# Four one-row products on four column tiles instead of one, and their copy in four pieces

## What is computed

```python
def _L1_attn_ref(x, Wq, bq, Wk, bk, Wv, bv):
    q = jnp.einsum('bsd,de->bse', x, Wq) + bq
    k = jnp.einsum('bsd,de->bse', x, Wk) + bk
    v = jnp.einsum('bsd,de->bse', x, Wv) + bv
    scores = jnp.einsum('bqd,bkd->bqk', q, k) / jnp.sqrt(jnp.asarray(d, x.dtype))
    attn = jax.nn.softmax(scores, axis=-1)
    return jnp.einsum('bqk,bkd->bqd', attn, v) + x
```

## Time and profile before

| | us |
|---|---|
| median of three runs | 3160.8 |
| lowest and highest | 3159.92, 3165.76 |
| the profiled execution, whole | 3153.07 |
| its span in the trace | 3151.5 |

### The profile page before, as it was taken

How to read it: one execution, slowest core, us unless ns; L and a number is a source line. 1 busy time by engine, 2 the same in 40 slices (tenths; PEclk the granted TensorE clock), 3 DMA queues, 4 the chain that set the end, 5 groups by cost and what they waited for, 6 DMA issues and landing times.

```text
span 3151.5 us, 69490 instructions
## 1 busy us (share of the span) xinstructions
PE 2865.8 (91%) x25025; PEld 1321.0 (42%) x25025; DVE 2418.2 (77%) x3155; ACT 2122.8 (67%) x3837; POOL 614.6 (20%) x493
## 2 busy tenths in 40 slices
PE   3788888888886899999999999999999999999997
PEld 3344444444443434343344344343343443443446
DVE  6788888888883887787787887877877877877844
ACT  2477767767764567776777777777777777777762
POOL 0344444444442010110110110100100101101100
PEclk6799999999998899999999999999999999999997
DMA  3000000000002901011011010010110110110003
GB/s 89 1 16 15 15 15 15 10 15 15 15 16 98 293 1 22 1 22 23 1 22 23 1 22 19 5 22 3 21 22 2 22 22 1 23 22 1 1 1 83
DMA packets 93922, 81.85 MB, mean 26 GB/s; under 512 B 62452, under 2 KB 83541, under 8 KB 92629
## 3 DMA queue, kind: packets, MB, share of 16 engines
q1 hardware_dynamic: 92085, 78.26, 9.5%
q10 hardware_dynamic: 1568, 0.04, 0.0%
HBM read 39.57 MB, written 32.11 MB: 23 GB/s over the span
## 4 chain that ended last, share of the span: by engine, by line
PE 67%; issue 11%; ACT 7%; POOL 6%; DVE 5%; DMA 2%; ACTq 1%; POOLq 0%; SPq 0%; DVEq 0%
PE ps L1635 19%; PE ps L1607 18%; PE ps L1659 17%; POOL arena L544 4%; PE ps L1669 3%; PE ps L1619 2%; POOL arena L550 2%; ACT arena L699 1%; PE ps L1487 1%; ACT L725 1%; ACT arena L817 1%; PE ps L1714 1%; DMA arena<-in_x 1%; POOL arena L560 1%; DVE arena L1052 1%
## 5 line engine op out<-in xcount | busy, mean ns | idle before, releaser
L1211 DVE TENSOR_REDUCE arena<-ps 128x2 f32<-128x896 f32 (+1 forms) x1408 | 1456.9, 1079 | 383.4 <-PE ps L1607 383.1
L837 ACT ACTIVATE arena<-ps 128x512 f32<-128x512 f32 (+1 forms) x2464 | 1281.3, 603 | 357.8 <-PE ps L1635 348.7
L1635 PE MATMUL ps<-arena 97*128 97x512 f16 (+1 forms) x2800 | 813.8, 357 | 13.5 <-ACT arena L817 10.6
L1607 PE MATMUL ps<-arena 96*128 96x448 f16 x2800 | 774.8, 359 | 21.5 <-issue 10.8
L1659 PE MATMUL ps<-arena 128*32 128x512 f32 (+2 forms) x7328 | 667.7, 457 | 0.7 <-DVE arena L1233 0.7
L1635 PEld LDWEIGHTS ps<-arena 97*128 97x128 f16 (+1 forms) x2800 | 252.2, 99 | 436.5 <-ACT arena L837 158.1
L1659 PEld LDWEIGHTS ps<-arena 128*32 128x32 f32 x7328 | 234.7, 109 | 411.3 <-ACT arena L837 195.6
L1607 PEld LDWEIGHTS ps<-arena 96*128 96x128 f16 x2800 | 224.1, 99 | 313.3 <-DVE arena L1211 130.9
L609 POOL TENSOR_TENSOR tok<-arena,tok 128x128 f32 (+3 forms) x112 | 47.4, 423 | 1574.6 <-DVE arena L1233 1574.6
L550 POOL TENSOR_TENSOR arena<-arena 113x784 f32<-113x784 f32 x128 | 192.4, 1503 | 429.5 <-DVE arena L1061 429.5
L544 POOL TENSOR_TENSOR arena<-arena 113x784 f32<-113x784 f32 x128 | 192.3, 1502 | 129.1 <-DVE arena L1052 129.1
(11 more groups left out here) (181 smaller groups left out, 2783.1 us busy)
## 6 DMA issues: line engine op xcount, KB each, us to landing
arena<-qk_scratch SPq DMA_DIRECT2D x96, 196.0 KB, 3.8
qk_scratch<-arena SPq DMA_DIRECT2D x16, 448.0 KB, 5.0
arena<-ximg SPq DMA_DIRECT2D x16, 400.0 KB, 6.7
arena<-in_x SPq DMA_DIRECT2D x4, 1568.0 KB, 8.3
xa_scratch<-arena SPq DMA_DIRECT2D x32, 196.0 KB, 1.9
res_scratch<-arena SPq DMA_DIRECT2D x32, 196.0 KB, 2.1
arena<-xa_scratch SPq DMA_DIRECT2D x4, 1568.0 KB, 8.0
arena<-res_scratch SPq DMA_DIRECT2D x4, 1568.0 KB, 11.7
```

What stands on the lines that cost most here:

```text
L837: act.activation(pk[0:rows, x % DEPTH, QC * m:QC * m + n], ps[0:rows, w % SB, 0:n], ACT.Exp, scale=float(C) ** -0.5).then_inc(att["exp"], 1)
L1211: dve.tensor_reduce(mxp[0:rows, p, 2 * u:2 * u + k], ps[0:rows, at_:at_ + k, 0:KN], AX_X, ALU.max)\
L1607: last = pe.matmul(ps[0:rows, MB + 2 * (j % 2) + n % 2, 0:KN], q2[p][0:96, T * t:T * t + rows], k2[p][0:96, KN * m:KN * m + KN], start=Tru ...
L1635: last = pe.matmul(ps[0:rows, bank, at_ % QC:at_ % QC + chunk_cols(c)], k2[p][0:97, T * t:T * t + rows], q2[p][0:97, QC * c:QC * c + chunk ...
```

## The change

The four products of a chunk no longer start at partition 96 all. Product i of four goes to partition 32 i, that is, to column tile i, in the same bank and the same columns as before. The row of maxima is then spread over four partitions, 0, 32, 64 and 96, with 128 columns in each, and ScalarE copies it in four instructions of 128 columns, each from its partition to partition 96 of `q2`. ScalarE waits once, ahead of the first, for the same signal `mrow` as before, and the last of the four signals `exp`. In the chunk of 64 the one product goes to partition 0 and is copied in one instruction from there. `C` is 32, `T` is 128.

```diff
             def max_row(b, p, c, w):
-                n = chunk_cols(c)
                 act.wait_ge(att["mrow"], b * NQ + c + 1)
-                act.activation(q2[p][96:97, QC * c:QC * c + n], ps[96:97, w % SB, 0:n], ACT.Copy).then_inc(att["exp"], 1)
+                for t in chunk_tiles(c):
+                    rows, i = tile_rows(t), t % 4
+                    last = act.activation(q2[p][96:97, T * t:T * t + rows], ps[C * i:C * i + 1, w % SB, T * i:T * i + rows],
+                                          ACT.Copy)
+                last.then_inc(att["exp"], 1)
...
                 for t in chunk_tiles(c):
                     rows, i = tile_rows(t), t % 4
                     at_ = 4 * ((NQ * p + c) % 2) + i
-                    last = pe.matmul(ps[96:97, w % SB, T * i:T * i + rows], mq[:, at_:at_ + 1], negid[:, 0:rows],
+                    last = pe.matmul(ps[C * i:C * i + 1, w % SB, T * i:T * i + rows], mq[:, at_:at_ + 1], negid[:, 0:rows],
                                      start=True, stop=True)
                 last.then_inc(att["mrow"], 1)
```

## The result

| | before | after |
|---|---|---|
| median, us | 3160.36 | 3200.98 |
| lowest and highest | 3150.37, 3165.76 | 3197.24, 3221.95 |
| span of the profiled execution | 3151.5 | 3195.6 |

The ratio is 1.0127, with a 95% interval of 1.0098 to 1.0157: the change makes the kernel slower, by 40.6 us in the medians. The forecast was 3200.

What follows compares the result with a forecast made beforehand. TensorE was taken to bound the kernel, waiting for the copy in 64 rows. Terms of 34.1, 3.2, 1.7 and 0.4 made 39.4 us: 3153.1 to 3192.5, with 7.7 up to the median forecast as 3200, range 3172 to 3213.

Steps and rivals of the forecast that it cites:

- The tight rows: 64 rows of chunks 1, 2, 4, 5: copy starts 0.01 us later, lasts 0.523 longer, TensorE waits: 34.1 us.
- The choice between the two neighbours: Copy pieces' spacing: taken from `pooled_copy` (no overlap, four take 1112 ns), not from line 865's overlapping copies.
- The lower bound, from line 865: Four copy pieces overlapping, a step of 0.155 us each, 0.73 together, 0.145 more than the one copy.
- Chunk 3: 16 rows: second score can start 0.40 us later, part replacing another wait; 0.2 each taken, 3.2 us, bounds 0 and 0.5.
- VectorE's full turn: In chunk 3's turn VectorE reduces four times without a break, 4.08 us, so part of the delay replaces that wait.
- Chunks 0 and 6: 31 rows beside key sums of four steps: a product on tile 0 adds its 0.055 us, 1.7 us in all.
- The cover of chunk 0's copy: Chunk 0's second score starts 2.45 us after x0, the pieces end at 2.28 (2.41 with the 0.13): copy hidden, thinly.
- The first row: The very first row, with no key sums around it, loses 0.4 us.
- The sum: Whole kernel: 39.4 us slower, profiled execution 3153.1 to 3192.5; with the median 7.7 above it, 3200.
- Overlapping pieces: Rival: ScalarE's copy pieces overlap as at line 865; 12 us slower, 3173; chance 0.13.
- The wait that isn't the copy: Rival: TensorE's gap before the second score is a tile switch, shorter key sums count; 8 us faster, 3153; chance 0.06.
- Program order: Rival: matmuls start in program order, so product 0 on tile 0 holds x1 back; 57 us slower, 3218; chance 0.05.

Runs made afterwards that it cites:

- e3: Kernel before, with products 0 and 1 on column tile 2, 2 and 3 on tile 3, and two copies of 256 columns: 3170.38 us, ratio 1.0035.
- e8: Kernel before, with two products each on column tiles 0 and 1 and the copy in two pieces: 3175.07 us beside 3160.63, one execution.
- e9: Kernel before, with three products on column tile 0, one on tile 3, copies of 384 and 128 columns: 3192.17 us beside 3160.63, one execution.
- e1: Kernel before, products still on column tile 3, the copy cut into four pieces of 128 columns, all from partition 96: 3172.11 us, ratio 1.0030.
- e7: Kernel before, with all four products on column tile 0 and the copy in four pieces, all from partition 0: 3220.0 us, ratio 1.0192.
- e2: Kernel before, products spread over four column tiles, still one copy from partition 96 (outputs not the reference's): 3160.31 us, ratio 0.9990.
- e4: Kernel before, with the row's products moved ahead of key sum x0 in program order, one tile, one copy: 3150.09 us, ratio 0.9958.
- e5: Kernel after, with the products moved ahead of key sum x0 in program order: 3160.64 us, ratio 0.9999 to the kernel before.
- e6: e3 with the products moved ahead of key sum x0 in program order: 3134.26 us, ratio 0.9908 to the kernel before.

## Why the prediction was right, step by step

**The tight rows** were forecast at 0.533 each, 34.1 us; the interval to the next row grew by 0.518, 33.2 us. The copy starts 5 ns later (forecast 10) and its pieces take 1.106 together (forecast 1.112). The step came from `pooled_copy`: 12 ns after the end of the one before, and e3 (386 and 374), e8 (383 and 372) and e9 (490 and 478) show 11 or 12. Nothing of the delay is caught up, as the step said.

**The choice between the two neighbours** carried the forecast, and e1 and e7 show it to be right for the reason given. The lower bound, from line 865, was 0.73 for four pieces; the four that stay in one group take 0.757 and 0.737. The Trainium skill, ScalarE: Activation LUTs, section "What ACT_TABLE_LOAD costs", has back-to-back ACTIVATEs overlap by about 93 ns: 90 to 92 in e1 and e7 agree, where the source group stays, and in the changed kernel there is no overlap at all. What the Trainium skill, VectorE: DVE Perf Modes, section "Two Vector instructions with no wait between them", says for VectorE of an input in another group of partitions is what these traces show of ScalarE's copies from PSUM. Its rule has a part on the output's group too; that group is the same from piece to piece in all of these runs, so no run here shows that part.

**Chunk 3** was mis-sized: 0.2 a row, 3.2 us, against 0.309, 4.9 us, inside the bounds of 0 and 0.5. The second score came 0.39 later, as said (0.40); what failed is the part that VectorE's full turn was to swallow. Here is the row of chunk 3 in the kernel after, beside the earlier trace rows:

```profile
1410.56 0.62 PE L1662 MATMUL ps<-arena 128*32 128x512 f32 x2
...
1411.73 1.11 ACT L818 ACTIVATE arena<-ps 1x128 f16<-1x128 f32 x4 [0.70 <-PE ps L1622]
1412.04 0.55 PE L1610 MATMUL ps<-arena 96*128 96x448 f16 x2
1412.62 1.09 DVE L1214 TENSOR_REDUCE arena<-ps 128x2 f32<-128x896 f32 x1 [0.65 <-PE ps L1610]
1412.96 0.60 PE L1638 MATMUL ps<-arena 97*128 97x512 f16 x2 [0.37 <-ACT arena L818]
1413.98 1.09 DVE L1214 TENSOR_REDUCE arena<-ps 128x2 f32<-128x896 f32 x1 [0.26 <-PE ps L1610]
```

Before, VectorE reduced four times without a break. Now it does the first, 0.15 earlier after x0, and then stands 0.26 until the scores behind the late second score arrive. The turn moves by the larger of two shifts: that of `produce`, and that of the second score less 0.079. The 0.079 is fitted to the kernel after; by it the others should move by 0, -0.148, -0.039, 0.685, 0.008 and 0.278 (e1, e2, e3, e7, e8, e9), and they moved by -0.005, -0.150, -0.036, 0.683, 0.010 and 0.276. In e4, e5 and e6 the products start 0.014, 0.055 and 0.013 ahead of x0; counted from the first product the rule gives -0.013, -0.171 and -0.119, and the turn moved by -0.014, -0.171 and -0.120. So the slack was 0.08, not half of 0.4; what in the turn makes it 0.08 was not followed further.

**Chunks 0 and 6** were forecast at 0.055 each, 1.7 us; measured 0.051 after chunk 0's row and 0.026 after chunk 6's (its product has 64 columns, not 128): 1.2 us. The cover of chunk 0's copy held: its second score starts 2.507 after x0 and 0.24 after the last piece's end, where it would have waited from 0.13 on. The row of chunk 0 in the kernel after, with the sums behind the copy (line 827):

```profile
1351.60 0.62 PE L1662 MATMUL ps<-arena 128*32 128x512 f32 x2
...
1352.76 1.10 ACT L818 ACTIVATE arena<-ps 1x128 f16<-1x128 f32 x4 [0.51 <-PE ps L1622]
1353.71 0.55 PE L1610 MATMUL ps<-arena 96*128 96x448 f16 x2
1353.89 0.60 ACT L827 ACTIVATE arena<-ps 128x512 f32<-128x512 f32 x1
1354.10 0.38 PE L1638 MATMUL ps<-arena 97*128 97x512 f16 x1
```

The sums start 2.29 after x0, where it was 2.21, and the second score comes as late after `produce` as in the other rows that wait for no copy (0.39).

**The first row** cost 0.22, not 0.4.

**The sum.** An image grew by 122.42 - 119.96 = 2.46 us, in 16 images 39.4, the forecast's figure: the miss at chunk 3 (1.7 too little) and those elsewhere (0.9, 0.5 and 0.2 too much) nearly cancel. The medians, 40.6 apart, agree with it. That the median after is within 1 us of the 3200 is in part luck: the four executions of before lie 15 us apart and those of after 25, and the 7.7 us between the profiled execution and the median, which the forecast added, is of the same kind (after: 3.7).

**The rivals.** Overlapping pieces fell by the 1.11. The wait that isn't the copy fell in e2, where the key sums end earlier and the tight rows gain nothing, and in e4, where the copy ends earlier and they gain 0.27. Program order fell for this kernel: x1 starts 0.075 after x0. But its ground was weaker than the prediction made it, which took from two rows that column tiles don't wait for each other's starts. The Trainium skill, TensorE: Matmul & The Clock Gate, section "Part 3: Packing small matmuls — row/col tiling", says that matmuls keep program order in start too; the trace contradicts it for the changed kernel, and e9 and e7 come close to it, with x1 held for 0.462 and 0.888. The kernel was spared because its products are one to a tile.

## What to carry to other kernels

Ask first what a copy waits for: here the products had ended 0.76 us before it started, held by a longer matmul ahead of them in the program, and moving them ahead of it took 12 us off the kernel before (e4), some 40 off the one after (e5) and some 35 off e3 (e6). When ScalarE copies small pieces one after the other, keep them in one partition group, or make few large ones: 128 columns cost a step of 0.28 us when the group changes and 0.16 to 0.18 when it doesn't. Spread work over column tiles for the sake of the tiles that end last, as e6 does with two, and not further than the copy behind it can hide.

## What the runs showed of the hardware that I had not expected

**Two matmuls may wait for a busy column tile, a third holds up all behind it.** x1's first pass, on free tiles and behind the products in the program, starts 27 ns after x0 with two products each for tiles 0 and 1 (e8), 75 with one on each tile (after), 462 with three for tile 0 (e9), and 888 with four (e7). The weight loads tell when it is let go. In e9, and then in e7, the loads for the products (PEld is the engine of weight loads):

```profile
1430.41 0.08 PEld L1623 LDWEIGHTS ps<-negid,mq 128*1 128x1 f16 x2 [0.31 <-ACT arena L840]
```

```profile
1434.06 0.08 PEld L1621 LDWEIGHTS ps<-negid,mq 128*1 128x1 f16 x1 [0.31 <-ACT arena L839]
1434.48 0.08 PEld L1621 LDWEIGHTS ps<-negid,mq 128*1 128x1 f16 x1 [0.34 <-issue]
```

In e9 the first of the three has its weights loaded at 0.46, and x1 goes at 0.462. In e7 the first of the four is loaded at 0.46 too, three are left, and x1 still stands; the second is loaded at 0.88, two are left, and x1 goes at 0.888. So x1 goes as soon as no more than two products are left whose weights aren't loaded. That this is the rule is inferred from these runs; other shapes were not tried.

**The end of the loop's body costs 1.6 to 7.3 us, and the larger sizes are the clock.** Two images share a body, and at its end TensorE waits with no releaser in the trace, 1.5 to 2.8 us, six times in a run. The first matmul behind that wait, before and after:

```profile
1470.95 0.55 PE L1607 MATMUL ps<-arena 96*128 96x448 f16 x2 [1.75 <-issue]
```

```profile
1478.17 0.55 PE L1610 MATMUL ps<-arena 96*128 96x448 f16 x2 [1.98 <-issue]
```

The images with this wait are longer than the others by 1.6 to 5.0 in before, 14.4 us in one execution, by 1.6 to 5.3 in after (20.9), by 5.1 to 7.3 in e4 (35.4), and by 3.7 to 5.6 in e6 (30.8). The granted clock tells the sizes apart. Here are the 20 us behind the first of the six waits of before and behind the second (start:end, length, PE, PEld, DVE, ACT, POOL, clock, DMA):

```profile
1471.00:1491.00 20.00, 20.00 (x147) 8.75 (x147) 14.84 (x19) 12.58 (x25) 0.70 (x2) 0.83 0.46 83
1716.00:1736.00 20.00, 19.81 (x173) 8.76 (x172) 16.56 (x21) 14.55 (x29) 0.70 (x2) 1.00 0.47 83
```

Behind the first wait the granted clock was 0.50, that is 1.2 GHz, for 6.8 us, and the image is 5.0 us longer. Behind the second it stayed at 1.00, and the image is 1.8 longer, about as much as TensorE stood (1.73). In all eleven traces every image that is more than 2.4 us longer has such a stretch behind its wait, and no other image has one: one of the six in before, three in after, five in e7, all six in e4 and e6. Why the clock falls behind one wait and not behind another stays open: it fell after TensorE had stood 1.60 us (e3) and not after 2.28 (e7).

So the profiled spans of before and after lie 44.1 apart, where 16 images make 39.4: 6.5 are these ends of the body, and the rest of the program took 1.8 less. It may also be why e4 gained 12 and not the 17.3 of its images; its profiled execution, with six falls of the clock, is the slowest of its six (3162.46), and the others have no trace. What the wait itself is for was not tried. The trace's two DMA queues of instructions moved seven packets in the 8 us around the first wait of before, and eight in the 86 us ahead of them; that TensorE waits for its instructions there would fit, and isn't shown.
